# Block numbers of the edge loop loaded in small groups, next to where they are used

## The chip, the core and the metric

The kernel runs on one core of one Trainium2 chip. The metric is device time in microseconds (us), the median over several executions. A profile is one further execution, taken with the hardware profiler; its times are of that execution alone.

## What is computed

The reference is one layer of a graph network over 6,250 nodes (256 values each) and 106,250 edges sorted by destination. Two attention convolutions over the edges, a linear attention over all nodes and a mixture of 8 experts are summed into the node values. The part that the change touches is the attention convolution, done twice:

```python
kj = k[src] + e          # e = edge_attr @ We
vj = v[src] + e
logits = einsum('ehc,ehc->eh', q[dst], kj) / sqrt(C)
m  = segment_max(logits, dst)
ex = exp(logits - m[dst])
a  = ex / (segment_sum(ex, dst)[dst] + 1e-16)
agg = segment_sum(vj * a[:, :, None], dst)
```

## The kernel before

Nodes lie in 49 blocks of 128. Edges lie in tiles of 128, one tile for each step. A tile that holds edges of two blocks is visited once for each block, so that one layer has 880 steps. A table `g.tab` in on-chip memory (SBUF) holds, for each step, the number of its edge tile (first half) and the number of its node block (second half, from `z.NSP` = 896 on).

The function `edges` does one layer. A chunk is T = 20 steps, a half chunk HT = 10, and the steps are done in pairs (q = 0 to 9 in a chunk, j = 2q the first step of the pair). Chunks 0 to 3 are written out, the next 40 are a hardware loop of 20 turns with two chunks each (p = 0 and p = 1), and two further ones drain the pipeline. Each engine has its own instruction stream, in program order, and the streams meet in semaphores:

- SyncE (SP) loads the edge attributes `ea` of each step, with tile numbers that it takes from the table ten at a time (L829).
- GpSimd (POOL) gathers the source nodes' keys and values `kv` (L859), one gather for each step, up to four pairs ahead of VectorE.
- TensorE (PE) multiplies `ea` by the weights (L916) and the one-hot of the destinations by the queries of the step's block (L919), both into `ps`, which has four slots. Which block it is comes from a register, used as an address (`g.q[:, bass.ds(blocks[j % HT], 1), ...]`). It may be two pairs ahead of VectorE.
- VectorE (DVE) does for each pair: `kj` (L1016), `vj` (L1028), `prod` (L1041), and the reduction of `prod` of the pair before (L977). Scans over the chunk's logits stand at fixed pairs: L1061 to L1063 at q = 2; the transpose L998 and then L1024, L1025 and L1034 to L1036 at q = 3; L1044 and L1056 at q = 4; L1019, L1020 and L1031 at q = 5. One-hots of ten steps (L961) stand at q = 0 and q = 5, the rescaling of a block (L1007) at q = 8.
- ScalarE (ACT) weighs `vj` (L897, L899), LAG = 36 steps after VectorE wrote it. TensorE sums it over destinations into `pa` (L938, two slots), and VectorE adds `pa` to the block's row of `acc` (`add`, L969), also 36 steps late. `add` needs the block number too. TensorE does L938 of a step only after the `add` two steps earlier.

A block number gets from the table into registers of one engine by `table` (L100 to L104). All of its instructions carry L102 in the profile: an address calculation (FUSED_REGOPS) and one TENSOR_LOAD that fills one or more registers. A row with a q behind the engine's name (DVEq, PEldq) is of the engine's sequencer, which takes the instructions in order, hands the arithmetic on to the engine and does the register instructions itself. Before the change

- TensorE loads ten numbers at each j % 10 == 0 (L912), before its products of that step,
- VectorE loads ten at q = 3 (L1000), behind the transpose L998 and ahead of the pair's first `add`; ten at q = 8 of the first chunk of a turn, or four in the second and in the written-out chunks (L1002); and six at q = 0 where nothing was kept from the chunk before (L995), that is at the start of each turn of the loop and of each written-out chunk.

Of the kernel before, what the change touches and what calls it, by code (L numbers as in the profile page):

```python
# [24 lines left out]
D = 256  # L25
# [12 lines left out]
T, HT, LAG, RV = 20, 10, 36, 40  # L38
# [706 lines left out]
def edges(nc, z, g, layer, a):  # L745
# [3 lines left out]
    with Stage(nc, f"edge{layer}") as st:  # L749
# [153 lines left out]
        def _(pe):  # L903
# [3 lines left out]
            def chunk(c, p, u, kept):  # L907
                for j in range(T):
                    s = c * T + j
                    if main(c):  # L910
                        if j % HT == 0:
                            blocks = table(nc, pe, g.tab[0:1, bass.ds(z.NSP + s, HT)], z.NB - 1)  # L912
                        pe.wait_ge(s_ea[j % HT], 32 * c + 16 * (j // HT) + 16)
                        need(pe, s_prod, c * HT + j // 2 - 1)
                        for k in range(2):
                            nc.tensor.matmul(ps[:, j % 4, 0:D], ea[:, j % HT, k, :], We[:, k, :], start=(k == 0), stop=(k == 1))  # L916
                        if j % HT == 0:
                            pe.wait_ge(s_oht, 2 * c + j // HT + 1)
                        nc.tensor.matmul(ps[:, j % 4, D:2 * D], oht[:, j // HT, (j % HT) * P:(j % HT + 1) * P],  # L919
                                         g.q[:, bass.ds(blocks[j % HT], 1), 0:D].rearrange("p o d -> p (o d)"), start=True, stop=True).then_inc(s_pe, 1)  # L920
                    if closed(c):
# [20 lines left out]
        def _(dve):  # L942
# [21 lines left out]
            def add(c, j, b):  # L964
# [5 lines left out]
                                               op0=ALU.mult, op1=ALU.add).then_inc(s_acc, 1)  # L970

            def reduce(c, p, q):
                s = 2 * q
                dve.wait_ge(s_prod, c * HT + q + 1)
                if q == 0:
                    need(dve, s_mt, c - 1)
                nc.vector.tensor_reduce(Lc[:, p, :, s:s + 2].rearrange("p h s -> p s h"),  # L977
                                        prod[:, q % 2, :, :].rearrange("p s (h k) -> p s h k", h=H), AX, ALU.add).then_inc(s_red, 1)

            def chunk(c, p, u, kept):  # L980
# [8 lines left out]
                for q in range(HT):  # L989
# [3 lines left out]
                    e = ps[:, bank, 0:D]  # L993
                    if q == 0 and here is None and lagged(c, 0):
                        here = [None] * 4 + list(table(nc, dve, g.tab[0:1, bass.ds(z.NSP + c * T - LAG, 6)], z.NB - 1))  # L995
                    if q == 3 and closed(c):
                        step(2)
                        nc.vector.transpose(TT[:, :], FB[:, 112:144]).then_inc(s_m, 1)  # L998
                    if q == 3 and lagged(c, j):
                        here = table(nc, dve, g.tab[0:1, bass.ds(z.NSP + c * T + j - LAG, HT)], z.NB - 1)  # L1000
                    if q == 8 and lagged(c, j):
                        here = table(nc, dve, g.tab[0:1, bass.ds(z.NSP + c * T + j - LAG, HT if not p and not isinstance(c, int) else 4)], z.NB - 1)  # L1002
                    if q == 8 and closed(c):
# [4 lines left out]
                    if lagged(c, j):  # L1008
                        if q == 8:
                            dve.wait_ge(s_resc, c)  # L1010
                        add(c, j, here[(j + 4) % HT])
                    if main(c):
# [16 lines left out]
                    if q == 5 and closed(c):  # L1029
                        step(12)  # L1030
                        nc.vector.tensor_scalar(Ym[:, :], mask4[:, :], dl[:, 0:1], None, ALU.mult).then_inc(s_Y, 1)  # L1031
                    if q == 3 and closed(c):
                        step(6)
# [3 lines left out]
                    if lagged(c, j + 1):  # L1037
                        add(c, j + 1, here[(j + 5) % HT])
                    if main(c):
# [683 lines left out]
```

## Time and profile before

| | |
|---|---|
| median of 3 executions | 5624.68 us (5619.65 to 5625.87) |
| the profiled execution, its own time | 5591.4 us |
| span of its records, first to last instruction | 5589.5 us |
| edge stage of layer 1, about | 475 to 2420 us |
| edge stage of layer 2, about | 2700 to 4610 us |
| TensorE, VectorE, ScalarE, GpSimd busy | 79%, 72%, 49%, 38% of the span |

The two edge stages are over two thirds of the span. An engine's busy time counts its arithmetic alone; what its sequencer does is not in it, and shows only as idle time of the engine, put down to "issue" where no semaphore ended it.

### The profile page before, as it was taken

The numbers are of one execution on the slowest core, as the hardware profiler recorded it, in microseconds if no ns is written. First come the engines' busy times: TensorE is split into PE (matmuls) and PEld (weight loads), VectorE is DVE, ScalarE is ACT, GpSimd is POOL, SyncE is SP. The second block draws the span as 40 slices with busy tenths as digits, with TensorE's granted clock in tenths as the row PEclk, the third lists the DMA queues.
The fourth block names the chain that finished last, engine by engine and source line by source line (L and its number), as shares of the span: only waits on it lengthen the run. The fifth ranks groups of instructions, "written<-read, shape, count | busy, mean of one in ns | idle before, by whom it ended". The sixth has DMA issues, their size and how long they took to land. (4 is left out here: it accounts for less than half of the span.)

```text
span 5589.5 us, 99514 instructions
## 1 busy us (share of the span) xinstructions
PE 4402.2 (79%) x18414; PEld 3403.3 (61%) x18415; DVE 4000.3 (72%) x8475; ACT 2763.5 (49%) x10075; POOL 2149.0 (38%) x2298
## 2 busy tenths in 40 slices
PE   3977988888888888878988888888888873139980
PEld 1546777777777777633777777777777752126650
DVE  4446988888888888854988888888888877302222
ACT  0122666666666666631566666666666661013320
POOL 1013544444444444300544444444444424430005
PEclk9999999999999999989999999999999985569995
DMA  4468666666666666534866666666666633432225
GB/s 94 135 217 243 187 182 187 185 181 186 182 191 189 180 187 182 150 112 148 235 185 185 182 181 188 182 183 183 179 186 180 186 102 101 173 97 64 64 78 153
DMA packets 617069, 919.99 MB, mean 165 GB/s; under 512 B 114486, under 2 KB 478582, under 8 KB 616535
## 3 DMA queue, kind: packets, MB, share of 16 engines
q0 software_dynamic: 154544, 502.26, 31.6%
q1 hardware_dynamic: 378966, 326.18, 20.9%
q10 hardware_dynamic: 83280, 89.03, 4.6%
q14 instruction: 251, 2.05, 0.1%
q8 instruction: 28, 0.46, 0.0%
HBM read 803.82 MB, written 113.31 MB: 164 GB/s over the span
## 5 line engine op out<-in xcount | busy, mean ns | idle before, releaser
L859 POOL DMA_INDIRECT edge_kv<-kvD,edge_ix x1760 | 1812.2, 1030 | 1914.7 <-DVE edge_vj L1028 1612.1
L897 ACT ACTIVATE edge_w<-edge_vj,edge_ex 128x64 f32<-128x64 f32 x7040 | 1864.8, 337 | 1012.4 <-PE edge_pa L938 903.6
L916 PE MATMUL edge_ps<-edge_We,edge_ea 112*128 112x256 f32 x7040 | 1906.6, 394 | 201.2 <-issue 173.9
L916 PEld LDWEIGHTS edge_ps<-edge_We,edge_ea 112*128 112x128 f32 x7040 | 1363.4, 196 | 495.5 <-issue 252.8
L938 PE MATMUL edge_pa<-edge_w,edge_oh 128*128 128x260 f32 x3520 | 1143.9, 409 | 309.2 <-DVE acc L969 298.9
L969 DVE SCALAR_TENSOR_TENSOR acc<-acc,flag,edge_pa 128x260 f32 x1760 | 839.2, 477 | 411.8 <-issue 320.7
L919 PE MATMUL edge_ps<-acc,edge_oht 128*128 x3520 | 1089.7, 391 | 0.0
L938 PEld LDWEIGHTS edge_pa<-edge_w,edge_oh 128*128 128x128 f32 x3520 | 647.7, 198 | 523.5 <-issue 322.4
L919 PEld LDWEIGHTS edge_ps<-acc,edge_oht 128*128 128x128 f32 x3520 | 697.8, 198 | 104.5
L1016 DVE TENSOR_TENSOR edge_kj<-edge_kv,edge_ps 128x512 f32<-128x512 f32 x880 | 600.0, 682 | 118.0 <-PE edge_ps L919 114.6
L1041 DVE TENSOR_TENSOR edge_prod<-edge_kj,edge_ps 128x512 f32<-128x512 f32 x880 | 598.6, 680 | 0.0
L1028 DVE TENSOR_TENSOR edge_vj<-edge_kv,edge_ps 128x512 f32<-128x512 f32 x880 | 597.3, 679 | 0.0
L977 DVE TENSOR_REDUCE edge_Lc<-edge_prod 128x8 f32<-128x512 f32 x880 | 597.2, 679 | 0.0
L470 PE MATMUL nodes_pj<-nodes_W,nodes_xT 128*128 128x512 f32 x784 | 361.7, 606 | 28.1 <-ACT nodes_xT L411 28.1
L899 ACT ACTIVATE edge_w<-edge_ex 128x4 f32<-128x4 f32 x1760 | 343.2, 195 | 0.0
L872 ACT ACTIVATE edge_oht<-edge_kb,edge_npart 128x1280 f32<-128x1280 uint8 x178 | 239.9, 1348 | 198.6 <-POOLq L858 101.4
L1544 DVE TENSOR_TENSOR exp_hb<-exp_pH,b 128x512 f32<-128x512 f32 x108 | 74.7, 692 | 325.9 <-PE exp_pH L1487 325.9
L961 DVE TENSOR_TENSOR edge_oh<-free,relS 128x1280 f32<-128x1280 f32 x176 | 260.8, 1482 | 0.0
L470 PEld LDWEIGHTS nodes_pj<-nodes_W,nodes_xT 128*128 128x128 f32 x784 | 144.3, 194 | 182.5 <-issue 146.0
L874 ACT ACTIVATE edge_oht<-edge_oht,ones 128x1280 f32<-128x1280 f32 x178 | 242.5, 1362 | 5.8
L542 DVE TENSOR_TENSOR acc<-nodes_pj,nodes_bias 128x256 f32 (+1 forms) x98 | 41.6, 425 | 236.2 <-PE nodes_pj L470 236.2
L1487 PE MATMUL exp_pH<-W,exp_xT 128*128 x432 | 205.3, 598 | 0.1
(230 smaller groups left out, 2878.6 us busy)
## 6 DMA issues: line engine op xcount, KB each, us to landing
edge_ea<-ea_t_dram SPq DMA_DIRECT2D x1760, 112.0 KB, 3.5
edge_kb<-relD SPq DMA_DIRECT2D x178, 160.0 KB
edge_kv<-kvD,edge_ix POOLq DMA_INDIRECT x1760, 4.4
kvD<-nodes_kvs ACTq DMA_DIRECT2D x98, 256.0 KB
xsD<-mix_zr POOLq DMA_DIRECT2D x27, 512.0 KB
exp_xr<-xsD SPq DMA_DIRECT2D x108, 128.0 KB, 2.1
ysD<-exp_yo ACTq DMA_DIRECT2D x108, 128.0 KB, 1.7
edge_pen<-penD SPq DMA_DIRECT2D x352, 32.0 KB
```

The source lines that it names most:

```text
L470: ins = nc.tensor.matmul(pj[:, j % 2, n * 2 * D:(n + 1) * 2 * D], xT[:, j, c, :], W[:, c, n * 2 * D:(n + 1) * 2 * D], start=(c == 0), stop ...
L859: nc.gpsimd.indirect_dma_start(out=kv[:, j % HT, :], out_offset=None, in_=g.kvD, in_offset=bass.IndirectOffsetOnAxis(ap=ix[:, h, j % HT:j ...
L897: nc.scalar.activation(w[:, j % 4, h * CA:h * CA + C], vj[:, slot, h * C:(h + 1) * C], ACT.Copy, scale=ex[:, x, h, k:k + 1])
L899: nc.scalar.activation(w[:, j % 4, :].rearrange("p (h k) -> p h k", h=H)[:, :, C], ex[:, x, :, k], ACT.Copy).then_inc(s_w, 1)
L916: nc.tensor.matmul(ps[:, j % 4, 0:D], ea[:, j % HT, k, :], We[:, k, :], start=(k == 0), stop=(k == 1))
L919: nc.tensor.matmul(ps[:, j % 4, D:2 * D], oht[:, j // HT, (j % HT) * P:(j % HT + 1) * P], g.q[:, bass.ds(blocks[j % HT], 1), 0:D].rearrang ...
L938: nc.tensor.matmul(pa[:, j % 2, 0:A], oh[:, par, (j + 4) % HT, :], w[:, j % 4, :], start=True, stop=True).then_inc(s_ape, 1)
L969: nc.vector.scalar_tensor_tensor(out=at, in0=at, scalar=g.flag[:, bass.ds(n, 1)], in1=pa[:, j % 2, 0:A], op0=ALU.mult, op1=ALU.add).then_i ...
L977: nc.vector.tensor_reduce(Lc[:, p, :, s:s + 2].rearrange("p h s -> p s h"), prod[:, q % 2, :, :].rearrange("p s (h k) -> p s h k", h=H), A ...
L1016: nc.vector.tensor_tensor(kj[:, q % 2, :, :], kv[:, both, 0:D], e, ALU.add).then_inc(s_kj, 1)
L1028: nc.vector.tensor_tensor(vj[:, p * T + j:p * T + j + 2, :], kv[:, both, D:2 * D], e, ALU.add).then_inc(s_vj, 1)
L1041: nc.vector.tensor_tensor(prod[:, q % 2, :, :], kj[:, q % 2, :, :], ps[:, bank, D:2 * D], ALU.mult).then_inc(s_prod, 1)
```

## The change

TensorE takes its block number in each step, one at a time, between the two products of the step. VectorE takes two numbers for each pair, in the pair before: behind `vj` (L1028) and, at q = 5, behind L1031, but ahead of the second `add`. Where nothing was taken ahead (the start of a turn and of a written-out chunk) it takes the two at the start of the pair. The number of steps, the arithmetic, the buffers and the semaphores stay.

```diff
@@ TensorE
                     if main(c):
-                        if j % HT == 0:
-                            blocks = table(nc, pe, g.tab[0:1, bass.ds(z.NSP + s, HT)], z.NB - 1)
                         pe.wait_ge(s_ea[j % HT], 32 * c + 16 * (j // HT) + 16)
                         need(pe, s_prod, c * HT + j // 2 - 1)
                         for k in range(2):
                             nc.tensor.matmul(ps[:, j % 4, 0:D], ea[:, j % HT, k, :], We[:, k, :], start=(k == 0), stop=(k == 1))
+                        block = table(nc, pe, g.tab[0:1, bass.ds(z.NSP + s, 1)], z.NB - 1)[0]
                         if j % HT == 0:
                             pe.wait_ge(s_oht, 2 * c + j // HT + 1)
...
-                                         g.q[:, bass.ds(blocks[j % HT], 1), 0:D].rearrange("p o d -> p (o d)"), start=True, stop=True).then_inc(s_pe, 1)
+                                         g.q[:, bass.ds(block, 1), 0:D].rearrange("p o d -> p (o d)"), start=True, stop=True).then_inc(s_pe, 1)
@@ VectorE
+            def blocks(n):
+                return table(nc, dve, g.tab[0:1, bass.ds(z.NSP + n, 2)], z.NB - 1)
+
...
-                    if q == 0 and here is None and lagged(c, 0):
-                        here = [None] * 4 + list(table(nc, dve, g.tab[0:1, bass.ds(z.NSP + c * T - LAG, 6)], z.NB - 1))
+                    if here is None and lagged(c, j):
+                        here = blocks(c * T + j - LAG)
                     if q == 3 and closed(c):
                         step(2)
                         nc.vector.transpose(TT[:, :], FB[:, 112:144]).then_inc(s_m, 1)
-                    if q == 3 and lagged(c, j):
-                        here = table(nc, dve, g.tab[0:1, bass.ds(z.NSP + c * T + j - LAG, HT)], z.NB - 1)
-                    if q == 8 and lagged(c, j):
-                        here = table(nc, dve, g.tab[0:1, bass.ds(z.NSP + c * T + j - LAG, HT if not p and not isinstance(c, int) else 4)], z.NB - 1)
...
-                        add(c, j, here[(j + 4) % HT])
+                        add(c, j, here[0])
...
                     if q == 5 and closed(c):
                         step(12)
                         nc.vector.tensor_scalar(Ym[:, :], mask4[:, :], dl[:, 0:1], None, ALU.mult).then_inc(s_Y, 1)
+                    if q == HT - 1 and (p or isinstance(c, int)):
+                        then = None
+                    elif lagged(c, j + 2):
+                        then = blocks(c * T + j + 2 - LAG)
+                    else:
+                        then = None
                     if q == 3 and closed(c):
                         step(6)
...
                     if lagged(c, j + 1):
-                        add(c, j + 1, here[(j + 5) % HT])
+                        add(c, j + 1, here[1])
+                    here = then
```

## Rows read from the trace of the kernel before

**Rows 1.** Windows inside the loops: stretch, length, busy PE, PEld, DVE, ACT, POOL, clock.

```profile
700.00:2200.00 1500.00, 1313.78 (x5647) 1076.10 (x5646) 1305.94 (x2647) 967.73 (x3655) 727.03 (x759) 0.96 0.66 185
2800.00:4500.00 1700.00, 1476.29 (x6340) 1210.33 (x6339) 1467.44 (x2980) 1083.44 (x4094) 814.58 (x850) 0.96 0.65 183
```

**Rows 2.** Waits of 700 to 2200 us: total us, times, longest.

```profile
DVE acc L969 <- issue: 124.7, 48, 3.1
...
DVE edge_kj L1016 <- PE edge_ps L919: 34.4, 55, 1.9
DVE acc L969 <- PE edge_pa L938: 23.6, 19, 2.3
DVE acc L969 <- DVE acc L1007: 10.5, 35, 0.3
```

**Rows 3.** Timeline of VectorE in one chunk: start, us, [idle before].

```profile
1501.85 0.48 DVE L969 SCALAR_TENSOR_TENSOR acc<-acc,flag,edge_pa 128x260 f32 x1 [2.70 <-issue]
...
1513.54 0.21 DVE L998 STREAM_TRANSPOSE edge_TT<-edge_FB 128x32 f32<-128x32 f32 x1
1516.27 0.48 DVE L969 SCALAR_TENSOR_TENSOR acc<-acc,flag,edge_pa 128x260 f32 x1 [2.52 <-issue]
...
1525.09 0.69 DVE L1016 TENSOR_TENSOR edge_kj<-edge_kv,edge_ps 128x512 f32<-128x512 f32 x1 [0.68 <-PE edge_ps L919]
...
1526.75 0.48 DVE L969 SCALAR_TENSOR_TENSOR acc<-acc,flag,edge_pa 128x260 f32 x1
...
1529.74 0.48 DVE L969 SCALAR_TENSOR_TENSOR acc<-acc,flag,edge_pa 128x260 f32 x1
...
1532.92 0.47 DVE L969 SCALAR_TENSOR_TENSOR acc<-acc,flag,edge_pa 128x260 f32 x1
```

**Rows 4.** VectorE's loads at L102 (ns min/median/max, first and last start us).

```profile
L102 DVEq TENSOR_LOAD <-tab x1: 837/837/837, 1500.7 to 1500.7; - x1
...
L102 DVEq TENSOR_LOAD <-tab x1: 2291/2291/2291, 1513.7 to 1513.7; - x1
...
L102 DVEq TENSOR_LOAD <-tab x1: 1061/1061/1061, 1534.1 to 1534.1; - x1
...
L102 DVEq TENSOR_LOAD <-tab x1: 349/349/349, 1575.9 to 1575.9; - x1
```

**Rows 5.** VectorE's sequencer: L986 before L998; L966, L290 in pair 7; L966 in pair 5.

```profile
L986 DVEq FUSED_REGOPS  x1: 53/53/53, 1510.9 to 1510.9; - x1
...
L966 DVEq ALU_OP  x1: 40/40/40, 1532.4 to 1532.4; - x1
...
L290 DVEq EVENT_SEMAPHORE  x1: 21/21/21, 1533.4 to 1533.4; - x1
...
L966 DVEq ALU_OP  x1: 40/40/40, 1526.2 to 1526.2; - x1
```

**Rows 6.** Loads of one number, of the expert stage, on VectorE and on TensorE.

```profile
L1541 DVEq TENSOR_LOAD <-etab x108: 300/305/318, 4975.2 to 5416.1; - x108
L1471 PEldq TENSOR_LOAD <-etab x216: 297/302/546, 4977.7 to 5420.3; - x108
```

**Rows 7.** TensorE: two loads of a chunk; L938, L916 behind gaps; sequencer's L919 and wait.

```profile
L102 PEldq TENSOR_LOAD <-tab x1: 2402/2402/2402, 1519.1 to 1519.1; - x1
L102 PEldq TENSOR_LOAD <-tab x1: 1092/1092/1092, 1539.2 to 1539.2; - x1
...
1516.90 0.68 PE L938 MATMUL edge_pa<-edge_w,edge_oh 128*128 128x260 f32 x2 [2.55 <-DVE acc L969]
...
1521.75 1.13 PE L916 MATMUL edge_ps<-edge_We,edge_ea 112*128 112x256 f32 x4 [1.12 <-issue]
...
L919 PEldq FUSED_REGOPS  x3: 55/55/55, 1521.9 to 1522.8; - x3
...
L290 PEldq EVENT_SEMAPHORE  x1: 51/51/51, 1545.6 to 1545.6; - x1
...
1545.66 0.84 PEld L916 LDWEIGHTS edge_ps<-edge_We,edge_ea 112*128 112x128 f32 x4
```

## The prediction, made before the changed kernel ran

> **What bounds the kernel now.** The page's busy shares come first: no engine is full. So I took windows inside the two loops, where the chunks repeat. VectorE is busy 1305.94 of 1500 us and 1467.44 of 1700 us; TensorE shows about the same, but its matmul records overlap [rows 1]. What an engine needs is clearer from weight loads: 1076.10 us, against VectorE's 1306. VectorE sets the pace, and what can be gained or lost is its idle time. The window holds 35 rescalings, one for each chunk [rows 2], so a chunk takes some 43 us, of which VectorE idles (1500 - 1305.94) / 35 = 5.5 us.
>
> The list of waits says what this idle time is: 124.7 us (48 times) in front of an `add` with no semaphore ending it ("issue"), 34.4 us for TensorE's L919 in front of `kj`, 23.6 us for L938, 10.5 us of the rescaling's own chain [rows 2]. The timeline of one chunk shows where the first stands: 2.52 us behind the transpose L998, and 2.70 us at the start of a turn [rows 3]. In the same places the sequencer's rows have the loads: 2.291 us for ten numbers from 1513.7 us (to 1516.0, with the `add` starting at 1516.27), 0.837 us for six from 1500.7 us. The load of ten at q = 8 takes 1.061 us from 1534.1 us [rows 4] and leaves no gap.
>
> Two things follow. First, the price of a load goes by the number of registers and by where it starts in the table. Four take 0.349 us, six 0.837, ten 1.061 or 2.291 [rows 4], one 0.305 on VectorE and 0.302 on TensorE [rows 6]. The cheap ones start at a multiple of four entries, the dear one (896 + 20c - 30) does not; there ten cost as much as one and nine more of (2.291 - 0.305) / 9 = 0.221. Second, the sequencer is hidden only while the engine has work queued. Before L998 it stood still from 1510.9 (L986) to 1513.6, since L998 waits for the scans just before it, and the load came behind that wait, with an empty engine [rows 3 to 5].
>
> Of this second point the Trainium skill (Perfetto Trace Analysis, section Per-engine timelines) says otherwise: a VectorE instruction is pushed into a wait queue, and the sequencer goes on. By it the load would have begun near 1511.0, not at 1513.7. The row decides here; by the page's rule the 34 us that I count as lost at q = 5 below would not be, and the time would be 5348 us.
>
> **The change, part by part.**
>
> *VectorE, q = 3.* The load of 2.29 us goes from behind L998. What is late next? The address work and the `add`: from the load's end (1516.0) to the `add` (1516.27) are 0.3 us, so the `add` can start 0.3 us after 1513.6, at 1513.88, against L998's end at 1513.75. Its TensorE input is no obstacle: the L938 that TensorE does next, 1516.90, waited for this very `add` [rows 7], and an L938 waits for the `add` two steps earlier, so this one's own input was there. The gap shrinks from 2.52 to 0.13 us. q = 3 has a load in 44 chunks of each layer: 88 x 2.39 = 210 us gained.
>
> *VectorE, start of a turn.* Six numbers (0.837) become two. The trace has no load of two. Bounds: not under the 0.305 of one, not over 0.305 + 0.244, where 0.244 is (0.837 - 0.349) / 2, the price of each of the two past the first four. I take 0.305 + 0.221 = 0.53, since the dear load is the one that goes register by register. The engine is empty there, so 0.31 us is gained, 40 times: 12 us. The rest of that gap is the jump back and what follows it, and stays. The loop's body gets some 15 loads longer; a gain is excluded, and as loss I take 0 to 0.3 us a turn (12 us) into the range.
>
> *VectorE, the loads of two.* 440 in each layer, against 112 loads before. Each costs its sequencer 0.065 + 0.53 and two small spacings, 0.67 us, ten times in a chunk: 6.7 us, against (0.84 + 2.29 + 1.06 + 2.29 + 0.35) / 2 = 3.4 before. Place matters, not sum. In a plain pair the sequencer has handed over `vj` by 1532.4 (L966) and then waits until 1533.4 (L290) for the first `add` to end [rows 5]. The load fits into this 1.0 us and costs nothing. If it did not fit, there is more: a plain pair takes 1532.92 - 1529.74 = 3.18 us [rows 3], the second `add` is due half of that after the first, at 1534.5, and its address work needs 0.3 us after 1533.4. At q = 3 the load stands before the wait of L1034 for the scan L1025, which covers it. At q = 8 L1007 delays the sequencer and the first `add` alike; I count nothing there. At q = 5 it is not covered: it stands behind L1031, which waits for L1020, and the sequencer gets free only at 1526.2 [rows 5], 0.55 us before the second `add` at 1526.75 [rows 3]. Of this it needs 0.3, so 0.25 covers a part of the 0.67: 0.4 us exposed, in 43 chunks of each layer: 86 x 0.4 = 34 us lost. Bounds: 0 (if the sequencer does pass a waiting L1031) and 0.67 (58 us).
>
> *TensorE.* Its loads of ten take 2.402 and 1.092 us, and the first is followed by 1.12 us of idle TensorE at 1521.75 [rows 7]. VectorE then waits for this step's L919: 0.68 us at 1525.09 [rows 3]. In the loop L919 costs VectorE 34.4 us for 35 chunks [rows 2], so 80 us for the 80 chunks of both loops. Moreover the pause at q = 3, in which TensorE too stands still (2.55 us), goes. I take two thirds as gone, 55 us; that is a choice between the bounds. Bounds: 0, and all of the 80 with the 55 that L938 costs by the same count (23.6 us for 35 chunks), so 135. The price of the single loads: 0.302 + 0.05 + spacing = 0.45 us in each step. Unhindered, TensorE's sequencer needs (1522.8 - 1521.9) / 2 = 0.45 us for a step [rows 7], so with the load 0.9 us, against the 8 weight loads of a step, (0.84 - 0.19) / 3 = 0.217 us apart by the four of 1545.66 [rows 7], so 1.74 us. And it runs ahead: it passes the wait of an L938 at 1545.6, when the four of L916 of that step only begin. The new load stands between the two products and is covered by the four weight loads of the first (0.84 us). I take nothing; bound above as the third rival.
>
> *Sum.* 210 + 12 + 55 - 34 = 243 us. From the profiled 5591.4 us that gives 5348. The median of the runs lies 33 us higher than the profiled execution, so from 5624.7 I predict **5382 us**.
>
> **A rule that speaks against the change.** A single number took a median of 0.30 us, in 324 loads [rows 6]. The Trainium skill (DMA: Bandwidth & Descriptors, section Latency and other measured facts) gives `tensor_load` a floor of about 600 ns and says that the compiler unrolls by four to share it; by that, splitting is dear. An estimate by that page: 0.3 us more for each load, so 26 us more lost at q = 5 and the 12 us at the turns' start not gained; the sum would be 205 us and the time 5420 us. Elsewhere a load of two of 0.97 us would still just fit into the 1.0 us.
>
> **The rivals.**
> 1. *As summed.* 5382 us, own range 5340 to 5440. Chance 0.62.
> 2. *TensorE's waits stay.* VectorE, 2.4 us a chunk quicker, catches up with TensorE, and the 55 us do not come, and somewhat more is lost: in plain pairs VectorE needs 3.18 us and TensorE 3.47. For: that inequality. Against: over a chunk VectorE has 1305.94 / 35 = 37 us of work to TensorE's 35, since the scans and one-hots come on top, and TensorE may be two pairs ahead. 5437, and to 5500 where 0.7 us a chunk are lost besides. Chance 0.18.
> 3. *TensorE becomes the bound*, because its single loads are not covered: 20 x 0.45 = 9 us a chunk on 35 gives 44 us. It costs from 5 us a chunk on, 0.25 a step, and turns the sign from 8 on, 0.4 a step. If all 9 show, a chunk takes a us longer than now: 88 us slower, 5713. Against: the 0.84 us of cover above. Chance 0.03.
> 4. *The pair loads are not hidden on VectorE* (the other side). If each cost what the one at q = 5 does, 10 x 0.4 x 88 = 352 us against 277 gained: 75 us slower, 5700. It turns the sign from 0.31 us a pair on. For: ten loads of 0.67 us stand on the engine that sets the pace. Against: the idle 1.0 us of the sequencer. Chance 0.05; half of it, 0.2 us a pair, gives 5524 and has 0.03.
> 5. *The sequencer passes a waiting instruction*, and all of TensorE's waits go. Nothing shows at q = 5: 210 + 12 + 135 = 357, 5268; with the 34 us alone, 5348. For: only that not every wait's place is seen. Against: the standstill before L998. Chance 0.07. (The wait queue of the Trainium skill's Perfetto Trace Analysis, Per-engine timelines, would do this.)
> 6. *No effect*, if something else ends the pause at q = 3, as the wait for L938. 0.02: TensorE's next step waited for this `add`.
>
> **How the numbers follow.** Faster by over 0.2% (11 us, what a measurement of this kernel can tell from no change): the first, second and fifth and the half of the fourth, 0.90. Within: the sixth, 0.02. Slower: the third and fourth, 0.08. The range leaves out the third, fourth and sixth and the far end of the fifth, and takes in what two bounds do together: 5300 to 5495.
>
> **What would show it.** Right: the gap before `add` behind L998 is 0.1 to 0.2 us; VectorE's loads x880 of about 0.53 us, TensorE's x1760 of 0.30; the `add` at q = 5 has a gap of 0.4 us put down to issue; L919's share of VectorE's waits is a third; a turn takes 5.5 us less. Wrong: "issue" gaps of 0.1 to 0.5 us in front of the second `add` of every pair (rival 4), or 0.1 to 0.4 us in front of TensorE's L919 in every step (rival 3), or a load that starts only when the engine is empty. The prediction fails first if a load of two takes much over 0.7 us, or if TensorE is late in plain pairs.

## The result and the profile after

| | before | changed |
|---|---|---|
| median of the runs | 5625.27 us (5619.65 to 5647.71, 4 runs) | 5292.56 us (5289.98 to 5295.89, 4 runs) |
| ratio, 95% interval | | 0.9402 (0.9376 to 0.9428) |
| profiled execution, own time | 5591.4 us | 5289.98 us |
| span of its records | 5589.5 us | 5288.2 us |

The kernel is 333 us faster by the medians (5625.27 - 5292.56) and 301 us by the profiled executions. The forecast was 243 us less, 5382; the result lies 7 us below the lower end of the range, 5300.

Two rows of the page hold VectorE's idle time in the edge loop, the two of before first (an `add` is L968 in the changed kernel, `kj` L1014). The columns are busy us, mean ns | idle us just before, and what ended most of it.

```profile
L969 DVE SCALAR_TENSOR_TENSOR acc<-acc,flag,edge_pa 128x260 f32 x1760 | 839.2, 477 | 411.8 <-issue 320.7
L1016 DVE TENSOR_TENSOR edge_kj<-edge_kv,edge_ps 128x512 f32<-128x512 f32 x880 | 600.0, 682 | 118.0 <-PE edge_ps L919 114.6
```

The same two rows of the changed kernel's page:

```profile
L968 DVE SCALAR_TENSOR_TENSOR acc<-acc,flag,edge_pa 128x260 f32 x1760 | 839.1, 477 | 178.8 <-issue 114.8
L1014 DVE TENSOR_TENSOR edge_kj<-edge_kv,edge_ps 128x512 f32<-128x512 f32 x880 | 599.0, 681 | 51.4 <-PE edge_ps L918 28.4
```

The busy time of both rows is the same; their idle time falls by 411.8 - 178.8 = 233 us and 118.0 - 51.4 = 66.6 us, together 300 us, as much as the 301 us of the profiled executions. "Issue" before the `add` lost 206 us.

The rest is mostly put down to TensorE. What ended the idle time in front of the `add`, over the whole span, before:

```profile
  issue: 320.7, 119
  PE edge_pa L938: 63.7, 80
  DVE acc L1007: 23.9, 80
```

and in the changed kernel:

```profile
  issue: 114.8, 118
  DVE acc L1005: 31.0, 80
  PE edge_pa L937: 22.9, 47
```

With the 114.6 and 28.4 us of the `kj` row, the profile puts 63.7 + 114.6 = 178 us of VectorE's waiting down to TensorE before and 22.9 + 28.4 = 51 us after: 127 us less. Not all of that is time won, because some gaps only change their label. So I also sorted the gaps by what VectorE did just before each, from the timelines of the whole span:

| where the gap stands | before, us | changed, us | difference |
|---|---|---|---|
| `add` behind the transpose, q = 3 | 216 | 8 | -208 |
| `add` behind the reduction, at the starts of turns and written-out chunks | 116 | 88 | -28 |
| second `add` of q = 5 | 0 | 28 | +28 |
| `add` and `kj` waiting for TensorE elsewhere | 148 | 49 | -99 |
| first `kj` of each layer | 19 | 19 | 0 |
| the chain of the rescaling | 24 | 31 | +7 |

The 8 us of the changed kernel are 88 gaps of 0.09 us, which I worked out from the one at 1121.56 below; the timelines don't mark gaps that short. The first `kj` of each layer stands as two waits for L919 (18.9 us) before and as "issue" (19.3 of the 22.0 us) after, and at the starts of turns 11 us are put down to L938 before and 2 us to L937 after. Without these two, VectorE's waits for TensorE fell by 99 us and not by 127. Of the 49 us that are left, 20 stand where the pipeline drains and most of the others in the first pairs of a layer. The largest loss that is left in the loop is the start of a turn, 88 us in all.

Windows inside the two loops of the changed kernel (length, busy PE, PEld, DVE, ACT, POOL, clock), to be held against [rows 1]:

```profile
700.00:2200.00 1500.00, 1392.39 (x6172) 1127.98 (x6170) 1422.41 (x2898) 1059.25 (x3988) 781.24 (x828) 1.00 0.72 202
2800.00:4200.00 1400.00, 1303.55 (x5774) 1053.93 (x5773) 1331.60 (x2715) 991.60 (x3727) 750.51 (x775) 1.00 0.72 202
```

And VectorE's waits in the first of them, against [rows 2]:

```profile
DVE acc L968 <- issue: 60.8, 56, 2.7
DVE acc L968 <- DVE acc L1005: 11.4, 38, 0.3
DVE edge_kj L1014 <- PE edge_ps L918: 2.0, 1, 2.0
```

38 rescalings in 1500 us make 39.5 us a chunk, where it was 42.9; VectorE idles (1500 - 1422.41) / 38 = 2.0 us of it, where it was 5.5. No wait for L937 is left in the loop, and one for L918 is all.

The timeline of VectorE shows where the "issue" is. In this order: the second `add` of q = 5 in the second chunk of a turn, the start of the next turn, the place behind the transpose (now L1000), and the second `add` of q = 5 in that turn's first chunk:

```profile
1090.82 0.48 DVE L968 SCALAR_TENSOR_TENSOR acc<-acc,flag,edge_pa 128x260 f32 x1 [0.61 <-issue]
...
1109.56 0.48 DVE L968 SCALAR_TENSOR_TENSOR acc<-acc,flag,edge_pa 128x260 f32 x1 [2.22 <-issue]
...
1121.26 0.21 DVE L1000 STREAM_TRANSPOSE edge_TT<-edge_FB 128x32 f32<-128x32 f32 x1
1121.56 0.48 DVE L968 SCALAR_TENSOR_TENSOR acc<-acc,flag,edge_pa 128x260 f32 x1
...
1131.07 0.23 DVE L1029 TENSOR_SCALAR edge_Ym<-edge_mask,edge_dl 128x4 f32<-128x4 f32 x1
1131.57 0.48 DVE L968 SCALAR_TENSOR_TENSOR acc<-acc,flag,edge_pa 128x260 f32 x1 [0.27 <-issue]
```

Of the 2.52 us behind the transpose [rows 3] 0.09 are left. At q = 5 there is a new gap: in layer 1 of 0.27 us in one chunk of a turn and 0.61 in the other, in layer 2 of 0.26 to 0.29 us in all; together 78 gaps and 28 us. No gap is marked in front of the second `add` of the other pairs.

The loads, over the whole span, on VectorE and on TensorE (ns min/median/max):

```profile
L102 DVEq TENSOR_LOAD <-tab x880: 523/529/772, 543.9 to 4289.8; - x176
```

```profile
L102 PEldq TENSOR_LOAD <-tab x1760: 295/302/496, 481.0 to 4250.8; - x196
```

### The profile page after: what moved, and what is told of

It is laid out like the page before. It is cut to its first block and busy times, and to the rows that moved or that the text cites. A ratio compares the mean times of both kernels' runs of the same rounds, so it can differ in the third digit from the quotient of the medians.

```text
span 5288.2 us, 103794 instructions
## 1 busy us (share of the span) xinstructions
PE 4326.9 (82%) x18414; PEld 3302.9 (62%) x18415; DVE 3988.7 (75%) x8475; ACT 2771.4 (52%) x10075; POOL 2147.1 (41%) x2298
## 5 line engine op out<-in xcount | busy, mean ns | idle before, releaser
L914 PE MATMUL edge_ps<-edge_We,edge_ea 112*128 112x256 f32 x7040 | 1839.6, 383 | 39.4 <-DMA edge_ea<-ea_t_dram 20.4
L914 PEld LDWEIGHTS edge_ps<-edge_We,edge_ea 112*128 112x128 f32 x7040 | 1317.4, 190 | 288.3 <-issue 82.3
L937 PE MATMUL edge_pa<-edge_w,edge_oh 128*128 128x260 f32 x3520 | 1119.8, 401 | 247.9 <-DVE acc L968 202.2
L918 PE MATMUL edge_ps<-acc,edge_oht 128*128 x3520 | 1056.3, 381 | 0.0
L968 DVE SCALAR_TENSOR_TENSOR acc<-acc,flag,edge_pa 128x260 f32 x1760 | 839.1, 477 | 178.8 <-issue 114.8
L937 PEld LDWEIGHTS edge_pa<-edge_w,edge_oh 128*128 128x128 f32 x3520 | 607.5, 190 | 532.9 <-ACT edge_w L899 288.5
L918 PEld LDWEIGHTS edge_ps<-acc,edge_oht 128*128 128x128 f32 x3520 | 674.4, 192 | 94.2
L1014 DVE TENSOR_TENSOR edge_kj<-edge_kv,edge_ps 128x512 f32<-128x512 f32 x880 | 599.0, 681 | 51.4 <-PE edge_ps L918 28.4
L853 POOL COPY edge_ix<-srcS 128x10 int32 (+1 forms) x176 | 35.1, 200 | 420.0 <-POOLq L84 419.1
```

What stands on the lines that cost most here:

```text
L937: nc.tensor.matmul(pa[:, j % 2, 0:A], oh[:, par, (j + 4) % HT, :], w[:, j % 4, :], start=True, stop=True).then_inc(s_ape, 1)
L968: nc.vector.scalar_tensor_tensor(out=at, in0=at, scalar=g.flag[:, bass.ds(n, 1)], in1=pa[:, j % 2, 0:A], op0=ALU.mult, op1=ALU.add).then_i ...
L1014: nc.vector.tensor_tensor(kj[:, q % 2, :, :], kv[:, both, 0:D], e, ALU.add).then_inc(s_kj, 1)
```

## The experiments

All times are medians; a ratio is to the kernel before in the same session, with its 95% interval. The kernel before had 5635, 5626 and 5604 us in the three sessions, so ratios compare across them and raw times don't.

**The two parts of the change alone.** `e1_vector_part` is the changed kernel with TensorE's loads of ten put back:

```diff
+                        if j % HT == 0:
+                            blocks = table(nc, pe, g.tab[0:1, bass.ds(z.NSP + s, HT)], z.NB - 1)
...
-                        block = table(nc, pe, g.tab[0:1, bass.ds(z.NSP + s, 1)], z.NB - 1)[0]
```

> VectorE's part of the change alone; TensorE loads ten numbers at each half chunk, as before. My theory now: the 300 us that the profile lost are 222 us of pauses behind L998 (88 of 2.52 us), less some 38 us at q = 5, some 30 at the turns' start, and the rest (about 85) time in which VectorE waited for TensorE. If that rest comes from TensorE's own two loads (2.40 and 1.09 us), this kernel keeps it: a gain of some 190 to 230 us, 5400 to 5440 us, with TensorE still idle for about 1 us (issue) in front of L916 twice a chunk. Rival: the rest comes from the pause at q = 3, after which TensorE comes late; then this kernel is as quick as the changed one, 5290 to 5320 us.

Measured: 5487.2 us, 0.9746 (0.9722 to 0.9770), a gain of 148 us. It keeps TensorE's waits, as the theory said, but gains less than the 190 to 230 us that I expected. `e2_tensor_part` has TensorE's single loads, and VectorE as before:

> TensorE's part alone; VectorE loads six, ten, ten and four as before, its load of 2.29 us behind L998 included. If TensorE's loads were what made VectorE wait, those waits (34.4 us for L919 in 1500 us) go and 60 to 110 us are gained: 5515 to 5565 us. Rival (the single loads cost TensorE, or its late products come from the pause): no gain, 5600 to 5640 us.

Measured: 5501.3 us, 0.9763 (0.9739 to 0.9786), a gain of 134 us, more than the 60 to 110 expected. VectorE's waits from 700 to 2000 us in `e1_vector_part`:

```profile
DVE acc L969 <- PE edge_pa L938: 44.8, 44, 2.1
DVE acc L969 <- issue: 35.4, 28, 2.9
DVE edge_kj L1015 <- PE edge_ps L919: 33.7, 33, 1.9
```

and in `e2_tensor_part`:

```profile
DVE acc L968 <- issue: 124.2, 59, 3.3
DVE acc L968 <- DVE acc L1006: 5.4, 18, 0.3
DVE edge_kj L1015 <- PE edge_ps L918: 4.7, 9, 1.9
```

With VectorE's part alone, "issue" shrinks and 78.5 us of waiting for TensorE stand in 31 chunks, 2.5 us a chunk, where [rows 2] have (34.4 + 23.6) / 35 = 1.7: VectorE arrives sooner and waits longer. The load of ten does more here than its own 2.4 us. TensorE and then VectorE, and TensorE's clock from 1505.0 to 1508.2 us, in `e1_vector_part` (the columns of the last row are those of [rows 1]):

```profile
1500.93 0.68 PE L938 MATMUL edge_pa<-edge_w,edge_oh 128*128 128x260 f32 x2
1503.71 1.13 PE L916 MATMUL edge_ps<-edge_We,edge_ea 112*128 112x256 f32 x4 [2.10 <-issue]
...
1506.29 1.91 PE L916 MATMUL edge_ps<-edge_We,edge_ea 112*128 112x256 f32 x4
...
1506.67 0.48 DVE L969 SCALAR_TENSOR_TENSOR acc<-acc,flag,edge_pa 128x260 f32 x1 [0.75 <-PE edge_pa L938]
1508.73 0.69 DVE L1015 TENSOR_TENSOR edge_kj<-edge_kv,edge_ps 128x512 f32<-128x512 f32 x1 [1.57 <-PE edge_ps L919]
...
1505.00:1508.20 3.20, 3.20 (x9) 2.56 (x8) 1.40 (x3) 1.62 (x6) 1.57 (x3) 0.50 0.66 175
```

A load of 2.411 us from 1501.1 us leaves TensorE idle for 2.10 us, then TensorE runs at 0.50 of its full clock, the lower level of 1.2 GHz, for some 3 us; four matmuls of L916 take 1.91 us there, where they take 1.03 us at the full clock (1508.96 us). VectorE's waits of 0.75 and 1.57 us stand in that stretch. How they divide between the idle time and the slow clock was not separated. The kernel before has the slow stretch too, but behind the pause at q = 3 (0.51 from 1517.8 to 1520.6 us), and its load of 2.402 us, from 1519.1 us, falls into it.

With TensorE's part alone those waits are all but gone, and the pause at q = 3 stays, with the slow stretch behind it (0.50 from 1539.0 to 1542.0 us): in spite of it VectorE waits for TensorE only 4.7 us in 1300. The parts add up to 282 us, 51 short of the 333. Each is worth more behind the other: TensorE's part gives 333 - 148 = 185 us once VectorE's is in, VectorE's 333 - 134 = 199 once TensorE's is. This is an account by medians of two sessions.

**The pause moved instead of split.** `e3_ten_moved` is the kernel before with one edit: VectorE's ten of q = 3 are loaded ahead of the transpose and the wait before it, not behind.

```diff
+                    if q == 3 and lagged(c, j):
+                        here = table(nc, dve, g.tab[0:1, bass.ds(z.NSP + c * T + j - LAG, HT)], z.NB - 1)
                     if q == 3 and closed(c):
                         step(2)
                         nc.vector.transpose(TT[:, :], FB[:, 112:144]).then_inc(s_m, 1)
-                    if q == 3 and lagged(c, j):
-                        here = table(nc, dve, g.tab[0:1, bass.ds(z.NSP + c * T + j - LAG, HT)], z.NB - 1)
```

> The kernel before with one edit: VectorE's load of ten at q = 3 stands ahead of the wait of L998, not behind it. Nothing is split. If the place was the fault and the size was not, the load of 2.29 us begins near where L986 began (2.6 us before L998), ends in time, and the pause of 2.52 us behind L998 goes nearly whole: 190 to 240 us gained, 5385 to 5435 us. Rival (the size is the fault; the sequencer cannot hide 2.29 us anywhere): the pause only moves, gain under 60 us.

Measured: 5477.7 us, 0.9731 (0.9704 to 0.9757), a gain of 158 us. That is less than the 190 to 240 expected, and as much as VectorE's whole part gives (148; the intervals overlap). The load still takes 2.3 us, but it runs while the scans do. The page's row of `kj` shows what is late next:

```profile
L1016 DVE TENSOR_TENSOR edge_kj<-edge_kv,edge_ps 128x512 f32<-128x512 f32 x880 | 600.1, 682 | 157.3 <-PE edge_ps L919 133.4
```

The wait for L919, 114.6 us before, is 133.4 us now: TensorE's load of 2.4 us is still there.

**The new gap at q = 5.** `e4_q5_ahead` is the changed kernel with the pair's load ahead of L1029 and the wait before it:

```diff
-                    if q == 5 and closed(c):
-                        step(12)
-                        nc.vector.tensor_scalar(Ym[:, :], mask4[:, :], dl[:, 0:1], None, ALU.mult).then_inc(s_Y, 1)
                     if q == HT - 1 and (p or isinstance(c, int)):
                         then = None
...
+                    if q == 5 and closed(c):
+                        step(12)
+                        nc.vector.tensor_scalar(Ym[:, :], mask4[:, :], dl[:, 0:1], None, ALU.mult).then_inc(s_Y, 1)
```

> The changed kernel with one edit: the load of two stands ahead of the wait of L1029 (Ym) at q = 5, not behind it. If the load there is exposed because it comes behind that wait, the gaps of 0.27 and 0.61 us in front of the second add at q = 5 go: 86 x 0.44 = 38 us quicker than the changed kernel, 5255 us. Rival (TensorE or ScalarE is next in line and takes it back): under 10 us quicker, 5283 to 5293 us.

Measured: 5256.1 us, 0.9330 (0.9304 to 0.9356), 37 us less than the changed kernel by the medians, (0.9402 - 0.9330) x 5635 = 41 by the ratios. Its waits from 700 to 2000 us have little but the turns' starts left under "issue":

```profile
DVE acc L968 <- issue: 42.8, 18, 2.9
```

Of the 18 gaps 17 are turns' starts, of 2.0 to 2.9 us each. So the sequencer does not pass a waiting L1029: moved ahead of it, the same load costs nothing. The changed kernel's trace shows what it waits for. L1029 needs the result of L1018:

```profile
1130.34 0.22 DVE L1018 SCALAR_TENSOR_TENSOR edge_dl<-edge_GX,edge_B 128x1 f32<-128x1 f32 x1
...
L102 DVEq FUSED_REGOPS  x2: 65/65/65, 1130.6 to 1132.5; - x2
```

L1018 ends at 1130.56 us, the load's address calculation begins at 1130.6, and L1029 itself starts only at 1131.07. Here the sequencer was held until L1018's result was there, not until L1029 ran.

**Two that did not do what they should.** `e5_vector_twice` and `e6_tensor_twice` were to double every load of a pair and of a step, the second copy unused.

```diff
             def blocks(n):
+                table(nc, dve, g.tab[0:1, bass.ds(z.NSP + n, 2)], z.NB - 1)
                 return table(nc, dve, g.tab[0:1, bass.ds(z.NSP + n, 2)], z.NB - 1)
```

> The changed kernel, with each of VectorE's loads of two done twice (the first result unused), so its sequencer has 1.2 us of loads in each pair instead of 0.67. My theory: a plain pair has about 1.0 us in which the sequencer waits for the first add, and 0.8 us more before the second add is due, so plain pairs stay hidden; only q = 5 (86 x 0.6 = 52 us) and the start of a turn (40 x 0.6 = 24) show: 5360 to 5375 us. Rival (the loads of two are near their limit and cost in every pair): over 0.3 us a pair, 5550 us and more.

> The changed kernel, with each of TensorE's single loads done twice. Theory: its sequencer then needs 0.45 + 0.45 + 0.45 = 1.35 us for a step, under the 1.74 us of weight loads: no change, 5285 to 5310 us. Rival (the single loads already cost TensorE): 0.2 us or more a step, over 300 us slower.

The traces have the loads x880 and x1760, no more than the changed kernel: the unused ones were dropped between the source and the chip. Measured: 5285.0 us, 0.9395 (0.9364 to 0.9425), and 5285.6 us, 0.9400 (0.9368 to 0.9431). They say nothing about cover, and serve as two repeats of the result. The question went to `e9_vector_five` and `e12_tensor_eight` below.

**Loads of four, aligned.** `e7_fours` is `e4_q5_ahead` with four numbers for every second pair on VectorE (behind q odd) and four at j % 4 == 0 on TensorE, always from a multiple of four:

```diff
-                        block = table(nc, pe, g.tab[0:1, bass.ds(z.NSP + s, 1)], z.NB - 1)[0]
+                        if j % 4 == 0:
+                            four = table(nc, pe, g.tab[0:1, bass.ds(z.NSP + s, 4)], z.NB - 1)
...
+                    elif q % 2 == 0:
+                        then = here[2:] if here is not None else None
```

> The changed kernel with the load at q = 5 ahead of the wait of L1029 (as in the run before), and fewer loads: four numbers from a start that is a multiple of four, on VectorE for two pairs, on TensorE for four steps. Theory: a load of four takes 0.35 us; what is hidden is hidden in either form, so only the start of a turn gains, 40 x 0.18 = 7 us: 5245 to 5260 us. Rival (the number of small loads costs something all over, by contention or in the sequencers): 30 us or more quicker, under 5230 us.

Measured: 5228.3 us, 0.9295 (0.9265 to 0.9325), the fastest time here, 57 us under the changed kernel's repeat `e5_vector_twice` of the same session. Against `e4_q5_ahead`, from which it differs by the fours alone, it is not clearly faster: the intervals overlap, and the profiled executions differ by 5257.4 - 5237.7 = 20 us. The theory had 5245 to 5260 us and the rival under 5230. The places of the gaps leave little to the rival: the starts of turns have 80 us where `e4_q5_ahead` has 94, and the chain of the rescaling 21 where it has 31. In the plain pairs neither has a gap to gain. Four numbers take 345 ns on VectorE and 332 on TensorE, less than two in the changed kernel (529):

```profile
L102 PEldq TENSOR_LOAD <-tab x440: 327/332/528, 481.6 to 4193.3; - x147
L102 DVEq TENSOR_LOAD <-tab x440: 339/345/608, 548.1 to 4234.9; - x147
```

**Nothing split, only aligned.** `e8_aligned_twelve` is the kernel before, its two dear loads of ten replaced by twelve from two entries earlier, a multiple of four:

```diff
-                        here = table(nc, dve, g.tab[0:1, bass.ds(z.NSP + c * T + j - LAG, HT)], z.NB - 1)
+                        here = table(nc, dve, g.tab[0:1, bass.ds(z.NSP + c * T + j - LAG - 2, HT + 2)], z.NB - 1)[2:]
```

(and likewise on TensorE at j == HT).

> The kernel before, with the two dear loads of ten (VectorE at q = 3, TensorE at j = 10) replaced in their places by loads of twelve that start two entries earlier, at a multiple of four. If the price goes by alignment (four together 0.35, each further four 0.22), twelve take 0.80 us instead of 2.29 and 2.40: the pause behind L998 falls from 2.52 to about 1.0 us, TensorE's gap in front of L914 or L916 at j = 10 goes nearly, and half to two thirds of the whole gain comes without moving or splitting: 5400 to 5470 us. Rival (the price goes by the number of registers): twelve take 2.7 us or more and the kernel is slower than before, 5660 us.

Measured: 5372.4 us, 0.9550 (0.9520 to 0.9581), a gain of 254 us, or three quarters of the whole; I had expected half to two thirds. Twelve aligned numbers take 0.86 us, where ten took 2.29 and 2.40. Waits from 700 to 2000 us:

```profile
DVE acc L971 <- issue: 75.7, 50, 3.0
DVE acc L971 <- DVE acc L1009: 9.0, 30, 0.3
DVE edge_kj L1018 <- PE edge_ps L921: 3.7, 8, 2.0
```

A load of 0.86 us on TensorE is already short enough: VectorE waits for L921 3.7 us in 1300, and for TensorE's other product not at all. On VectorE it still stands behind the transpose's wait, and 1.08 us of the pause remain. `e11_twelve_moved` takes that away too, by the move of `e3_ten_moved`:

```diff
+                    if q == 3 and lagged(c, j):
+                        here = table(nc, dve, g.tab[0:1, bass.ds(z.NSP + c * T + j - LAG - 2, HT + 2)], z.NB - 1)[2:]
                     if q == 3 and closed(c):
                         step(2)
```

> The kernel before with aligned twelves in place of the two dear tens (measured 5372 us) and, besides, VectorE's twelve of the third quarter moved ahead of the step's weights add; no load is split. Theory: the pause of 1.08 us behind L1000 goes, 88 x 1.0 = 88 us, so about 5285 us, level with the changed kernel. Rival (the move only shifts the wait to TensorE's products, as when the tens were moved): 5340 us or above.

Measured: 5263.7 us, 0.9395 (0.9379 to 0.9411): the changed kernel's gain, with no load split. (Expected were 5285 us.) The page's row of the `add` keeps 168.3 us idle, against 178.8 in the changed kernel:

```profile
L971 DVE SCALAR_TENSOR_TENSOR acc<-acc,flag,edge_pa 128x260 f32 x1760 | 833.6, 474 | 168.3 <-issue 102.7
```

**TensorE: the price or the number?** `e10_tensor_twelve` has the changed kernel's VectorE, and on TensorE ten for the first half chunk and an aligned twelve for the second:

```diff
+                        if j == 0:
+                            blocks = table(nc, pe, g.tab[0:1, bass.ds(z.NSP + s, HT)], z.NB - 1)
+                        if j == HT:
+                            blocks = table(nc, pe, g.tab[0:1, bass.ds(z.NSP + s - 2, HT + 2)], z.NB - 1)[2:]
```

> The changed kernel's VectorE part, with TensorE loading not one number a step but the ten of the first half chunk (start a multiple of four) and an aligned twelve in place of the ten of the second (0.86 us in place of 2.40). Theory (it was the price of TensorE's dear load that VectorE paid for, not that ten come at once): about 5290 us, within 20 of the changed kernel. Rival (the loads must be split, the block of about 1 us is still too long for TensorE to stay ahead): near VectorE's part alone, 5400 us or above.

Measured: 5280.9 us, 0.9418 (0.9402 to 0.9434), against 0.9746 in `e1_vector_part`, which differs from it by one load in a chunk: ten at 2.40 us in place of twelve at 0.86. So it is the price of that load, and not that ten or twelve come at once. Its waits from 700 to 2000 us:

```profile
DVE acc L971 <- issue: 29.7, 38, 2.7
DVE acc L971 <- PE edge_pa L940: 23.1, 11, 2.4
DVE acc L971 <- DVE acc L1008: 9.6, 32, 0.3
DVE edge_kj L1017 <- PE edge_ps L921: 3.8, 16, 0.3
```

The 23.1 us for L940 are 11 gaps at the starts of turns, of about 2 us each, where the changed kernel has gaps of the same size under "issue"; all four rows together are 66 us, as the changed kernel's are.

**How much cover a pair has on VectorE.** `e9_vector_five` loads five numbers for each pair, from one entry before, and uses two:

```diff
-                return table(nc, dve, g.tab[0:1, bass.ds(z.NSP + n, 2)], z.NB - 1)
+                return table(nc, dve, g.tab[0:1, bass.ds(z.NSP + n - 1, 5)], z.NB - 1)[1:3]
```

> The changed kernel with VectorE's load for a pair widened from two numbers to five, from the number before the pair's two, so that it never starts at a multiple of four; it still uses two. Price by the rows: between the two-number load (0.53 us) and the ten-number one off a multiple of four (2.30), some 1.2 us. Theory (a load is hidden while it ends before the pair's products are ready, which leaves about 1.8 us of VectorE's work in a pair): plain pairs stay hidden; only the places where the sequencer is held grow, by 0.66 us each: the second add of a chunk +57 us, the turn's start and the eighth quarter +26 each at most, so about 5395 us. Rival (the loads of the pairs already sit at the limit of their cover): at least 0.3 us more in each of the 880 pairs, 5550 us or above.

Measured: 5426.7 us, 0.9689 (0.9668 to 0.9709). The load takes 1.18 us in place of 0.53. By ratios that is 161 us slower than the changed kernel, by the spans 5426.1 - 5288.2 = 138; expected were some 105. The waits from 700 to 2000 us:

```profile
DVE acc L968 <- issue: 97.3, 93, 3.7
DVE acc L968 <- DVE acc L1005: 9.3, 31, 0.3
DVE edge_R L1038 <- issue: 3.9, 16, 0.3
```

93 gaps in 31 chunks are three to a chunk, not ten. The timeline has them at the second `add` of q = 5, at the turn's start and the `add` behind it, and at the second `add` of q = 8. Elsewhere next to no gap is marked: the plain pairs hide 1.18 us too, as the theory said. It had the turn's start too small: that gap is 3.22 us, 1.0 more than the 2.22 above, and 0.34 us follow at the next `add`:

```profile
1126.77 0.48 DVE L968 SCALAR_TENSOR_TENSOR acc<-acc,flag,edge_pa 128x260 f32 x1 [3.22 <-issue]
...
1128.78 0.48 DVE L968 SCALAR_TENSOR_TENSOR acc<-acc,flag,edge_pa 128x260 f32 x1 [0.34 <-issue]
```

**How much cover a step has on TensorE.** `e12_tensor_eight` loads eight numbers in each step and uses one:

```diff
-                        block = table(nc, pe, g.tab[0:1, bass.ds(z.NSP + s, 1)], z.NB - 1)[0]
+                        block = table(nc, pe, g.tab[0:1, bass.ds(z.NSP + s, 8)], z.NB - 1)[0]
```

> The changed kernel with TensorE's load of each step widened to eight numbers, of which it uses one: a quarter of them start at a multiple of four (some 0.57 us), the others don't (some 1.85), about 1.5 us in the mean in place of 0.30. The rival of the prediction in which TensorE's sequencer becomes the bound: its work for a step rises to about 2.0 to 2.1 us, above the 1.74 us that VectorE takes of a step at present, so the kernel becomes 150 to 250 us slower than the changed one, 5440 to 5540, and VectorE waits for TensorE at each pair. Other theory (weight loads and register loads of the sequencer run beside each other, so nothing is paid): within 20 us of 5290.

Measured: 5820.4 us, 1.0386 (1.0369 to 1.0404). The direction was right, the size was not: 530 us over the changed kernel by the spans, not 150 to 250. Weight loads of two steps, with the idle time before them:

```profile
1203.30 0.41 PEld L937 LDWEIGHTS edge_pa<-edge_w,edge_oh 128*128 128x128 f32 x2
1203.74 0.84 PEld L914 LDWEIGHTS edge_ps<-edge_We,edge_ea 112*128 112x128 f32 x4
1205.59 0.30 PEld L918 LDWEIGHTS edge_ps<-acc,edge_oht 128*128 128x128 f32 x2 [1.01 <-issue]
```

and the sequencer's loads in that stretch:

```profile
L102 PEldq TENSOR_LOAD <-tab x14: 592/1934/1942, 1198.3 to 1228.5; - x14
```

The load of this step runs from 1203.5 to 1205.4 us. L914's four weight loads end at 1204.58, and L918's start at 1205.59: a load of 1.93 us leaves 1.01 us of idle TensorE, 0.9 us of it was covered, about the four weight loads of L914 (0.84 us), and the rest shows. My expectation had added the sequencer's work up over a step, as if the loads could spread under all eight weight loads; with this place of the load the cover is the one product before it. Another place was not tried.

## Why the prediction was off

**Right, by the steps.** The pause at q = 3: 2.52 us became 0.09, which is 208 us; the sum had 88 x 2.39 = 210. The prices of the loads: 0.529 us for two and 0.302 for one, forecast 0.53 and 0.30. The place of the loss at q = 5, and nearly its size: 28 us, forecast 34; `e4_q5_ahead` gave 37 us back by the medians and 33 by the profiled executions. Plain pairs hide the load of two, and with room to spare (`e9_vector_five`). TensorE's single loads are covered by L914's weight loads; those give 0.9 us (`e12_tensor_eight`), and 0.45 is used.

**The step that failed** is TensorE's term of the sum: "I take two thirds as gone, 55 us; that is a choice between the bounds". The mechanism was the right one, its size was not. VectorE's waits for TensorE fell by 127 us as the page labels them and by 99 us sorted by place, and inside the loop they fell to one wait of 2 us. By the runs TensorE's part is worth 134 us alone and 185 us behind VectorE's.

- The 55 us were two thirds of the 80 us for L919 alone; of the 55 us for L938 nothing was taken, and no reason was given for either. The upper bound of 135 us was not too low for what fell. It was not clean either: in the 23.6 us for L938 of [rows 2] are gaps at turns' starts, of 2.1 to 2.3 us each (2.23 at 1063.97 us), and gaps there are in the changed kernel too, under "issue".
- The trace had a reason to take the whole: the load of 2.402 us, followed by 1.12 us of idle TensorE and 0.68 us of waiting VectorE, beside one of 1.092 us with nothing behind it [rows 7]. `e10_tensor_twelve` shows that this one load is all of it: cut to 0.86 us, with ten and twelve numbers still loaded at once, what is left are 3.8 us for L921 in 1300 and the turns' starts.
- The prediction did not count TensorE's clock. Each idle stretch of 2.1 to 2.6 us on TensorE that I looked at was followed by some 3 us at the lower level, in the kernel before as in `e1_vector_part`. In `e1_vector_part` VectorE waits just there. The change removes these idle stretches and the slow ones with them (0.96 before and 1.00 after, from 700 to 2200 us), and what each is worth stays open.

A smaller term was low too: the start of a turn, 12 us forecast and 28 us found (3.05 us in the mean became 2.27, over 38 turns). The load there became 0.31 us shorter, as forecast, which is the 12 us; what the other 16 us are was not tried. By place, in the profiled executions: 208 + 28 - 28 + 99 - 7 (the rescaling's chain) = 300 us, against 301 measured and 210 + 12 - 34 + 55 = 243 forecast. Of the difference 44 us are TensorE's.

**The median.** I carried over that the median lay 33 us above the profiled execution. The changed kernel's profiled execution is at 5290 us, its median at 5293. The kernel before ranged from 5591 to 5648 us over all its executions, the changed one, with its two repeats, from 5281 to 5296. By the profiled executions alone the forecast of the gain was 58 us off, by the medians 90; so some 30 us of the miss are no step of the sum, but the place of one profiled execution among the others. Why the kernel before spreads more was not tried.

**The rivals.** The second (TensorE's waits stay) was refuted by the waits row; with TensorE's loads of ten put back its mechanism is there (`e1_vector_part`, 2.5 us of waiting a chunk where there were 1.7). The third and fourth (single loads, pair loads not hidden) did not occur; `e12_tensor_eight` and `e9_vector_five` show at what price of a load they begin. The fifth had the time nearest to the result (5268), but its mechanism is refuted: the sequencer does not pass a waiting L1029, so that its number came near is luck; and its other half, all of TensorE's waits gone, needed no such passing. I had tied the two together, and so gave the full 135 us only 0.07. The sixth (no effect) is refuted by the time. The rule that spoke against the change, 0.3 us more for each load, did not hold either: 1760 loads of one took 0.302 us and 880 of two 0.529 us in the median.

**Which part of the change gained.** The split is not what was needed. `e8_aligned_twelve` has 254 of the 333 us by the start of two loads alone, and `e11_twelve_moved` the whole (0.9395 to the changed kernel's 0.9402) with one more line moved. Split loads of one and two are one way to have no dear load, and no long one behind a wait.

## What to carry to other kernels

Read the duration of each register load beside its start in the table: here ten numbers off a multiple of four cost 2.3 to 2.4 us and twelve on it 0.86, so loading more can be the cheaper load. A load belongs ahead of a wait, where the engine still has queued work over it (`e3_ten_moved`, `e4_q5_ahead`), and on TensorE, placed between the products, its cover was the product just before it. Where a wait on a partner engine has one visible cause that the change removes, take the whole wait and not a share of it, and sort the gaps by what stands just before each: the label of a gap can change while the gap stays.

## What the runs showed of the hardware

- The time of a register load goes by count and start: one takes 0.30 us wherever it starts; two take 0.53 (the pairs' loads start on a multiple of four every other time; median 0.529, lowest 0.523); five off a multiple of four take 1.18, eight 0.59 on it and 1.93 off it, ten 1.06 to 1.09 on it and 2.29 to 2.40 off it; on it four take 0.33 to 0.35 and twelve 0.86. Twelve on it being quicker than ten on it suggests that a remainder of two is dear; this was not tried.
- A register load of VectorE that stands behind an instruction with an unmet wait begins when the wait is met: at 1130.6 us, with L1018 ending at 1130.56 and L1029 starting at 1131.07.
- The granted TensorE clock in the loop (window 700 to 2000 us) was 0.96 in the kernel before and in `e2_tensor_part`, 0.97 in `e1_vector_part` and `e3_ten_moved`, 0.99 in `e9_vector_five`, and 1.00, all of the 2.4 GHz, in the changed kernel and in `e4_q5_ahead`, `e7_fours`, `e8_aligned_twelve`, `e10_tensor_twelve`, `e11_twelve_moved` and `e12_tensor_eight`. Where it is lower, it is so in stretches of some 3 us at 0.50, behind gaps of TensorE of 2.55 us (the kernel before), 2.10 (`e1_vector_part`) and 2.45 (`e9_vector_five`). `e12_tensor_eight`, the slowest kernel of all, has weight loads wait for up to 1.2 us in most steps and keeps 1.00. Part of the 51 us by which the two parts together gain more than one by one may be this; it was not separated.
- Unused register loads do not reach the chip, so a load can't be doubled by writing it twice (`e5_vector_twice`, `e6_tensor_twice`).
